# Gate weights loaded into the first attention's old tiles, and each weight's difference and sum as separate steps

## The chip, the cores and the metric

The kernel runs on one core of a Trainium2 chip. It is one launch that computes two transformer blocks. Its time is the device time of a whole execution in microseconds (us); 771.56 us is the median of three runs (771.15 to 772.16).

## The reference

`x` is 2 x 1024 tokens of 256 values. Two blocks follow each other, and in each the attention and the feed-forward part (ffn) read the same normalised input:

```python
xn = layernorm(x)
x = x + attn0(xn) + ffn0(xn)       # linear attention; ffn with ternary weights
xn = layernorm(x)
x = x + attn1(xn) + ffn1(xn)       # softmax attention, 16 heads, RoPE; Hadamard ffn
# ffn1:
x = fwht(x * SU_ug) / 64
up, gate = x @ W_up.T * ws[:1024] * 64, x @ W_gate.T * ws[1024:] * 64
x = fwht(silu(gate) * up * SU_dp) / 64
y = x @ W_down.T * (Wscale_dp * 64)
```

The Hadamard transform `fwht` of the input can be moved onto the weights: instead of transforming every token, the kernel transforms W_up and W_gate once (256 rows each, for 1024 outputs). A transform over 256 rows is one over 128 rows, done as a matmul with a 128x128 Hadamard matrix, of the sum and of the difference of the two halves of 128 rows. Sum and difference are what this change is about.

## The kernel before

**Precision.** Weights and activations are used as a rounded high part and the rest as a low part (names ending in H and L), so that a product is two or three matmuls. In ffn terms: a `gate` or `up` of the first ffn is four L748 matmuls of 512 columns into one PSUM bank, a `down` eight L754 matmuls of 256 columns into banks 6 and 7.

**Order.** There is no dynamic scheduling. `work_order` writes one list of pieces by hand; each engine walks through this list and does its part of each piece, and semaphores join them. The main line is the first ffn: four chunks of 512 tokens, in each of them m = 0 to 7 with `gate`, `up` and, three behind, `down`. A side line (`side0`) is woven in: first the first attention, then the preparation of the second block's weights (`prep_attn1`, `prep_down` 0 to 3, `prep_ug` 0 to 7), then the query and key projections of the second attention (`qk`). Preparation stands beside chunk 2 from m = 6 and chunk 3 up to m = 3 of the first ffn.

**One m of the first ffn.** TensorE `gate`; ScalarE tanh into `sg` (L1457); VectorE multiplies with the gate (L1239), which frees that bank; VectorE multiplies with `up` (L1248, "the product"), which frees the other; ScalarE copies into `hh` (L1465); GpSimd makes the low part `hl` (L1591, `low_part`); `down` reads both. Gates and ups rotate through the banks 3, 4, 5; the side line through 0, 1, 2.

**The preparation.** `prep_ug` u (L871 to L878) is one matmul with the Hadamard matrix, u = 0 to 3 for the up weights and 4 to 7 for the gate weights: two with the sum, two with the difference. ScalarE writes the high part UGH (L1445), VectorE the low part UGL (L1274), which frees the bank. Sum and difference are made on GpSimd by `halves_ug` (L1572 to L1581): both in one piece, difference (L1579) and sum (L1581, in place). `prep_attn1` (ScalarE, L1431) takes the high parts of the second attention's weights from the staging tile `stg[1]`, `low_attn1` (GpSimd, L1583 to L1587) their low parts, and signals `w1l`. The first `qk` waits for `w1l` to reach 2.

**Loads.** They go through SP's queue in the order of the list. `load_up` (L643) brings the up weights to `stg[0]`, once the down weights have left it. `load_gate` (L647) brings the gate weights to `stg[1]`, once `low_attn1` is done. `load_cs` (L633) is behind it and brings the tables for RoPE.

The order of the list around the change, ffn pieces with (chunk, m): `up` (2,5), `down` (2,2), `ln_norm` 5, `bias` (1,1), `att_b`, `gate` (2,6), `prep_attn1`, `up` (2,6), `prep_down` 0, `down` (2,3), `ln_turn` 5, `gate` (2,7), `prep_down` 1, `up` (2,7), `halves_ug` 0, `prep_down` 2, `down` (2,4), `low_attn1`, `load_gate`, `prep_down` 3, `down` (2,5), `prep_ug` 0, `down` (2,6), `down` (2,7), `halves_ug` 1, `prep_ug` 1, `ffn_end`, `gate` (3,0), `load_cs`, `prep_ug` 2, `up` (3,0), `prep_ug` 3, `gate` (3,1), `prep_ug` 4, `up` (3,1), `gate` (3,2), `prep_ug` 5, `up` (3,2), `prep_ug` 6, `gate` (3,3), `prep_ug` 7, `up` (3,3), `qk` 0, `down` (3,0), `ln_stats` 6.

Of the kernel before, what the change touches and what calls it, by code (L numbers as in the profile page):

```python
# [8 lines left out]
ALU = mybir.AluOpType  # L9
# [30 lines left out]
""".split()  # L40

DMAS = """
cols idn c ob wsd x0 x1 x2 x3 st0 st1 cs pad sp0 sp1 sp2 sp3 km0 km1 qm0 qm1 ks0 ks1 qs0 qs1 m0 m1
oe0 oe1 num0 num1 rc0 rc1 rs0 rs1 late0 late1 late2 late3 wl y
""".split()

# [19 lines left out]
def work_order():  # L66
# [3 lines left out]
    def put(*piece):  # L70
        order.append(piece)
# [139 lines left out]
    def side0():  # L211
        bf = 0
        for n, _ in enumerate(attention0()):
            if 14 <= n < 18:
                next(tn)
                if n == 17:
                    put("scales")
                    put("spread_vb")
                    put("load_wa1")
            if n == 18:  # L220
                put("fold")
            if n == 30:
                put("add_vb", ps.next())
            if n >= 18 and n % 3 == 1 and bf < 6:
                put("butterfly", bf)
                bf += 1
                if bf == 6:
                    put("load_up")
            yield
        ps.slots.append(2)  # L230
        put("prep_attn1")
        yield
        for q in range(4):
            put("prep_down", q, ps.next())
            yield
            if q == 1:
                put("halves_ug", 0)
            if q == 2:
                put("low_attn1")
                put("load_gate")  # L240
        for u in range(8):
            put("prep_ug", u, ps.next())
            yield
            if u == 0:
                put("halves_ug", 1)
        for c in (0, 1):
            for n in range(2):
                yield from qk(c, n, 4)
        put("load_m", 0)
        put("load_m", 1)  # L250
# [25 lines left out]
    for i in (1, 2):  # L276
        next(ln0[i])
    put("signs")
    sd0 = side0()
    next(sd0)  # L280
    next(ln0[2])
# [89 lines left out]
    st, mxr = Ring([0, 1, 2, 3]), Ring([4, 5, 6])  # L371
# [10 lines left out]
    while s < 8 * NP + LAG or any(k >= s for k in plan):  # L382
        live = s < 8 * NP
        for piece in plan.get(s, []):
            if piece[0] == "recip":
                p = piece[1]
# [21 lines left out]
        if 0 <= s - LAG < 8 * NP:  # L408
# [4 lines left out]
            elif t % 8 == 7:  # L413
                p = t // 8
# [18 lines left out]
def program(nc, x_d, wa0, tern, wa1, wo1, wf1, cols_d, bkv_d, cos_d, sin_d, had_d, mask_d, ident_d, pad_d, sel_d, wl_d, ob_d, wsd_d, y_d):  # L433
    with ExitStack() as ctx:
        base = -(-nc.sbuf_base // 32) * 32

        def sb(name, kb, shape, dt=F32):
            return nc.alloc_sbuf_tensor_at(name, shape, dt, offset=base + int(kb * KB))

        q = {n: ctx.enter_context(nc.semaphore(f"s_{n}")) for n in SEMAPHORES}  # L440
        d = {n: ctx.enter_context(nc.semaphore(f"d_{n}")) for n in DMAS}
# [4 lines left out]
        cols = sb("cols", 24, [128, NCOL])  # L446
# [14 lines left out]
        W1H = sb("W1H", 60, [128, 2, 768], F32R)  # L461
        W1L = sb("W1L", 66, [128, 2, 768], F32R)
        WOH = sb("WOH", 80, [128, 2, 256], F32R)
        WOL = sb("WOL", 82, [128, 2, 256], F32R)
# [21 lines left out]
        stg = [sb(f"stg{i}", 174 + 8 * i, [128, 2048]) for i in range(2)]  # L486
        XC = [sb(f"XC{i}", (190, 194, 156, 160)[i], [128, 4, 256]) for i in range(4)]
        XD = [sb(f"XD{i}", (16, 20, 198)[i], [128, 4, 256]) for i in range(3)]
        stg2 = sb("stg2", 190, [128, 2048])
        DIF = [sb(f"DIF{i}", (198, 190)[i], [128, 1024]) for i in range(2)]  # L490
        OB = sb("OB", 202, [128, 256])
        WSD = sb("WSD", 203, [128, 256])
        rz = [sb(f"rz{i}", 207 + i / 8, [128, 2, 8]) for i in range(2)]
# [37 lines left out]
        def r32(ap):  # L531
            return ap.bitcast(F32)
# [24 lines left out]
        def slot_value(p):  # L557
# [1 line left out]


        STAGE = {"wa0": (0, 16), "tern0": (1, 16), "tern1": (0, 32), "tern2": (1, 32), "down": (0, 48), "wa1": (1, 64),
                 "up": (0, 64), "gate": (1, 80)}

        def o_slots(p):

# [39 lines left out]
        def _(e):  # L605
# [39 lines left out]
                e.dma_start(stg[0][:, :], wf1[0]).then_inc(d["st0"], 16)  # L645

            def load_gate():  # L647
                e.wait_ge(q["w1l"], 2)
                e.dma_start(stg[1][:, :], wf1[1]).then_inc(d["st1"], 16)

            def qk_split(c, n):
                i = 2 * c + n
# [65 lines left out]
            def last(banks):  # L718
                for i in range(2):
                    for cc in range(2):  # L720
# [4 lines left out]
            parts = {f.__name__: f for f in (start, load_wa0, load_ob1, tern_abs, load_down, load_cs, load_wa1, load_up, load_gate, qk_split, load_m, load_s, max_rows,  # L725
                                             load_wl, out, recip, project, last)}
# [6 lines left out]
        def _(e):  # L733
# [134 lines left out]

            def prep_ug(u, b):
                n, k, h = u // 4, u // 2 % 2, u % 2  # L870
                src = DIF[n] if k else stg[n][:, 0:1024]  # L871
                claim(b)
                if h == 0:
                    e.wait_ge(q["hs"], 2 * n + 2)
                e.matmul(bank[b], HAD[:, :], src[:, h * 512:(h + 1) * 512], start=True, stop=True).then_inc(q["pu"], 1)
                freed[b] = q["ul"], u + 1
# [148 lines left out]
            def last(banks):  # L1025
# [32 lines left out]
                for i, qs in enumerate(halves):  # L1058
                    e.wait_ge(q["ll"], i + 1)
                    for cc in range(2):  # L1060
                        for r in range(2):
# [4 lines left out]
            parts = {f.__name__: f for f in (start, ln_turn, tern_scale, kv_in, kv_out, q0, att_n, att_t, att_b, add_vb, prep_down, prep_ug,  # L1066
                                             gate_a, gate, up_a, up, down_a, down, ffn_end, qk, v, max_half, max_rows, scores, values, project, last)}
# [312 lines left out]
        def _(e):  # L1380
# [94 lines left out]
            def qk_split(c, n):  # L1475
                i = 2 * c + n
                rot, spl = rots[c // 2], spls[c // 2]
                sc = 0.25 if n == 0 else 1.0
                for m in range(2):
                    e.wait_ge(q["rg"], 2 * i + m + 1)  # L1480
                    if i == 0:
                        e.wait_ge(q["pu"], 4)
                    else:
                        e.wait_ge(d[f"sp{2 * m}"], 32 * i)
                    e.activation(spl[2 * m][:, :], rot[m][:, :], ACT.Copy, scale=sc).then_inc(q["sh"], 1)  # L1485
# [30 lines left out]
            def last(banks):  # L1516
# [6 lines left out]
                for i, qs in enumerate(halves):  # L1523
# [3 lines left out]
            parts = {f.__name__: f for f in (start, ln_stats, ln_turn, w0h, tern_abs, kv_in, q0, att_t, prep_attn1, prep_down, prep_ug, gate, up,  # L1527
                                             hidden, qk_split, v, max_rows, scores, out, load_exp, last)}
# [5 lines left out]
        def _(e):  # L1534
# [34 lines left out]
                a, z = (x.rearrange("p (o t i) -> p o t i", t=2, i=256 << k // 2) for x in (pair if k // 2 % 2 == 0 else pair[::-1]))  # L1569
                e.tensor_tensor(z[:, :, k % 2, :], a[:, :, 0, :], a[:, :, 1, :], ALU.subtract if k % 2 else ALU.add).then_inc(q["bf"], 1)  # L1570

            def halves_ug(n):  # L1572

                i, value = STAGE["up" if n == 0 else "gate"]
                lo, hi = stg[i][:, 0:1024], stg[i][:, 1024:2048]
                e.wait_ge(d[f"st{i}"], value)
                if n == 1:
                    e.wait_ge(q["pd"], 4)
                e.tensor_tensor(DIF[n][:, :], lo, hi, ALU.subtract).then_inc(q["hs"], 1)  # L1579
                e.wait_ge(q["hs"], 2 * n + 1)  # L1580
                e.tensor_tensor(lo, lo, hi, ALU.add).then_inc(q["hs"], 1)  # L1581

            def low_attn1():  # L1583
                for i, (o, n, H, L) in enumerate(((0, 768, W1H, W1L), (1536, 256, WOH, WOL))):
                    raw = stg[1][:, o:o + 2 * n].rearrange("p (k n) -> p k n", k=2)
                    e.wait_ge(q["w1h"], i + 1)
                    e.tensor_tensor(L[:, :, :], raw, r32(H[:, :, :]), ALU.subtract).then_inc(q["w1l"], 1)  # L1587

            def low_part(f):
                e.wait_ge(q["hh"], f + 1)  # L1590
# [69 lines left out]
                    e.memset(DEN[1][96:128, :], 1.0).then_inc(q["fill"], 1)  # L1660
                    e.wait_ge(q["fill"], 2)

            parts = {f.__name__: f for f in (bias, fold, kv_in, q0, butterfly, low_attn1, halves_ug, up, hidden, ones_v, qk_join, load_wl, out, recip, times, high, low)}
            for name, *args in order:
                if name in parts:
                    parts[name](*args)
# [83 lines left out]
```

## Time and profile before

| | |
|---|---|
| median of three runs | 771.56 us (771.15 to 772.16) |
| the profiled execution | 771.74 us, of it 769.9 us span |
| TensorE matmuls busy | 705.2 us, 92% of the span |
| VectorE, ScalarE, GpSimd busy | 549.1, 434.9 and 299.3 us |
| chain that ended last | 59% TensorE |
| preparation of the ffn weights (`prep_ug` 0 to 7) | 204.7 to 228.2 us |
| mean granted clock | 0.965 of full speed |

Times in the rows are microseconds from the start of the span. An engine's busy time counts its instructions; matmuls overlap, so that the distance from one start to the next is shorter than the duration shown. In brackets stands the idle time before an instruction and what ended it. The granted clock is 1.00 at 2.4 GHz and 0.50 at 1.2 GHz.

### The profile page before, as it was taken

What the parts mean: (1) busy time and instruction counts of PE and PEld (TensorE: products, weight loads), DVE (VectorE), ACT (ScalarE), POOL (GpSimd) and SP (SyncE); (2) the same over time, 40 slices, a digit from 0 to 9 for tenths busy, and PEclk for the clock granted to TensorE, in tenths of its full rate; (3) what the DMA queues carried; (4) which work ended last, traced back from release to release, by engine and by line L of the source; (5) the groups of instructions that cost most, each with busy time, mean ns of one, the idle gap of its engine ahead of it and who ended that gap; (6) DMA issues with size and microseconds to landing.
All of it is one profiled execution on the core that took longest, in us unless ns stands there. A gap on an engine that the chain in (4) does not pass through costs nothing.

```text
span 769.9 us, 10969 instructions
## 1 busy us (share of the span) xinstructions
PE 705.2 (92%) x4186; PEld 442.3 (57%) x4186; DVE 549.1 (71%) x895; ACT 434.9 (56%) x579; POOL 299.3 (39%) x277
## 2 busy tenths in 40 slices
PE   3778898969687998999999998999999999999998
PEld 3657797958456777867767676333333433333345
DVE  4897766676368676667878888888888378888415
ACT  2542323344344554243233334899999899999883
POOL 0157865332644585354254343022233213422520
PEclk7798999998899999999999999999999999999999
DMA  6136101000021356342311102344344245342231
GB/s 250 55 114 228 55 1 55 1 1 0 19 91 44 122 187 201 107 148 70 111 55 56 56 5 69 110 139 136 107 138 139 91 134 172 123 138 84 78 102 59
DMA packets 25704, 74.14 MB, mean 96 GB/s; under 512 B 4604, under 2 KB 5980, under 8 KB 24692
## 3 DMA queue, kind: packets, MB, share of 16 engines
q1 hardware_dynamic: 21124, 65.37, 25.4%
q0 software_dynamic: 3808, 7.60, 3.3%
q8 instruction: 33, 0.54, 0.3%
q10 hardware_dynamic: 720, 0.48, 0.2%
q14 instruction: 19, 0.16, 0.1%
HBM read 54.54 MB, written 23.06 MB: 101 GB/s over the span
## 4 chain that ended last, share of the span: by engine, by line
PE 59%; POOL 2%; DVE 2%; ACT 2%; issue 1%; DMA 0%; SPq 0%; DVEq 0%; ACTq 0%; POOLq 0%
PE PS L1010 16%; PE PS L748 12%; PE PS L996 11%; PE PS L754 8%; PE PS L979 6%; PE PS L969 4%; DVE mx L1310 1%; POOL sg L1600 1%; ACT P L1503 1%; POOL rot L1620 0%; POOL rot L1621 0%; DMA scr_k<-spl 0%; PE PS L985 0%; ACT spl L1485 0%; ACT us L1468 0%
## 5 line engine op out<-in xcount | busy, mean ns | idle before, releaser
L1503 ACT ACTIVATE P<-PS 128x1024 f32<-128x1024 f32 x256 | 249.1, 1023 | 30.9 <-PE PS L996 30.6
L1317 DVE TENSOR_REDUCE mx<-PS 128x1 f32<-128x512 f32 x300 | 189.1, 682 | 33.2 <-PE PS L979 31.6
L1310 DVE TENSOR_REDUCE mx<-PS 128x2 f32<-128x1024 f32 x106 | 124.8, 1220 | 37.4 <-PE PS L969 37.1
L1591 POOL TENSOR_TENSOR hl<-sg,hh 128x512 fp32r<-128x512 f32 x64 | 83.4, 1304 | 140.0 <-ACT hh L1465 73.8
L1010 PE MATMUL PS<-P,VV 128*32 128x512 f32 x1024 | 137.3, 608 | 0.1
L996 PEld LDWEIGHTS PS<-QS,KS 64*128 64x128 f32 x512 | 48.6, 183 | 124.0 <-ACT P L1503 110.9
L996 PE MATMUL PS<-QS,KS 64*128 64x512 f32 x512 | 117.0, 456 | 2.3 <-DVE mx L1310 1.8
L979 PE MATMUL PS<-KM,QM 64*128 64x512 f32 x300 | 81.7, 398 | 0.0
L1459 ACT ACTIVATE sg<-PS,cols 128x512 f32<-128x512 f32 x32 | 22.0, 689 | 80.4 <-PE PS L748 80.4
L1600 POOL TENSOR_TENSOR sg<-sg,us 128x512 f32<-128x512 f32 x32 | 42.1, 1316 | 39.5 <-ACT us L1468 39.5
L748 PE MATMUL PS<-XH,UGH 128*128 128x512 f32 x128 | 54.3, 424 | 2.1 <-ACT sg L1459 1.1
L748 PE MATMUL PS<-XL,UGH 128*128 128x512 f32 x128 | 50.5, 394 | 0.0
L748 PE MATMUL PS<-XH,UGL 128*128 128x512 f32 x128 | 49.9, 390 | 0.0
L1465 ACT ACTIVATE hh<-sg 128x512 fp32r<-128x512 f32 x32 | 20.2, 630 | 51.5 <-DVE sg L1248 51.5
L1010 PEld LDWEIGHTS PS<-P,VV 128*32 128x32 f32 x1024 | 20.3, 108 | 39.8 <-issue 34.9
L1239 DVE SCALAR_TENSOR_TENSOR sg<-sg,PS 128x512 f32<-128x512 f32 x32 | 21.8, 682 | 26.6 <-ACT sg L1457 26.5
L969 PE MATMUL PS<-KM,QM 64*128 64x512 f32 x212 | 39.9, 448 | 0.8 <-DVE mx L1310 0.6
L979 PEld LDWEIGHTS PS<-KM,QM 64*128 64x128 f32 x300 | 38.2, 186 | 3.5 <-DVE mx L1317 0.6
L754 PE MATMUL PS<-DH,hh 128*128 128x256 f32 x128 | 38.0, 297 | 0.0
L1457 ACT ACTIVATE sg<-PS,s 128x512 f32<-128x512 f32 x32 | 21.8, 682 | 27.6 <-PE PS L748 27.5
L754 PE MATMUL PS<-DL,hh 128*128 128x256 f32 x128 | 36.2, 282 | 0.0
L754 PE MATMUL PS<-DH,hl 128*128 128x256 f32 x128 | 36.1, 282 | 0.0
(205 smaller groups left out, 1404.3 us busy)
## 6 DMA issues: line engine op xcount, KB each, us to landing
QM<-scr_q SPq DMA_DIRECT2D x16, 512.0 KB, 4.3
KM<-scr_k SPq DMA_DIRECT2D x16, 512.0 KB, 5.3
QS<-scr_q SPq DMA_DIRECT2D x16, 512.0 KB, 4.3
KS<-scr_k SPq DMA_DIRECT2D x16, 512.0 KB, 5.1
scr_q<-spl SPq DMA_DIRECT2D x24, 256.0 KB, 3.3
scr_k<-spl SPq DMA_DIRECT2D x24, 256.0 KB, 3.3
scr_o<-OE POOLq DMA_DIRECT2D x14, 256.0 KB, 2.8
stg<-in_tern SPq DMA_DIRECT2D x3, 1024.0 KB, 4.8
```

What stands on the lines that cost most here:

```text
L748: i = e.matmul(out, l, r, start=start and j == 0, stop=stop and j == len(pairs) - 1)
L754: i = e.matmul(out[:, r * 256:r * 256 + 256], l, x, start=first and r == 0 and j == 0, stop=last and j == len(pairs) - 1, skip_group_check ...
L969: e.matmul(bank[b + h], QM[p % 2][hr, qt * 128:(qt + 1) * 128], KM[p % 2][hr, chunk(half)], start=True, stop=True).then_inc(q["mt"], 1)
L979: e.matmul(bank[b], QM[p % 2][hr, qt * 128:(qt + 1) * 128], KM[p % 2][hr, chunk(half)], start=True, stop=True).then_inc(q["mt"], 1)
L996: i = e.matmul(bank[b + h], KS[p % 2][hr, kt * 128:(kt + 1) * 128], QS[p % 2][hr, chunk(half)], start=True, stop=True)
L1010: i = e.matmul(PS[32 * c:32 * c + 32, 7, :], v_head(8 * b + kt, 2 * j + c // 2), P[s % 4][:, chunk(c // 2 + 2 * (c % 2))], start=(kt == 0) ...
L1310: e.tensor_reduce(mx[p % 2][:, :, qt, half], PS[:, b:b + 2, :], AX.X, ALU.max).then_inc(q["mx"], 2)
L1317: e.tensor_reduce(mx[p % 2][:, h, qt, half:half + 1], bank[b], AX.X, ALU.max).then_inc(q["mx"], 1)
L1459: e.activation(s[:, :], bank[b], ACT.Silu, scale=col("wsg", m)).then_inc(q["t"], 1)
L1503: e.activation(P[s % 4][:, half * 1024:(half + 1) * 1024], PS[:, b:b + 2, :].rearrange("p b n -> p (b n)"), ACT.Exp).then_inc(q["ex"], 1)
L1591: e.tensor_tensor(hl[f % 4][:, :], sg[f % 3][:, :], r32(hh[f % 4][:, :]), ALU.subtract).then_inc(q["hl"], 1)
L1600: e.tensor_tensor(s[:, :], s[:, :], us[f % 4][:, :], ALU.mult).then_inc(q["h"], 1)
```

## The change

- `load_gate` moves to the place behind `prep_attn1`. It waits for eight of the first attention's query pieces and for all sixteen `att_n`, and brings the gate weights in two DMAs to two new tiles GR, at 128 to 132 and 136 to 140 KB, where tiles of the first attention lay. The second GR tile and the first are later overwritten by UGL, each after it has been read.
- `halves_ug` is split into `difference` n and `total` n, four steps. `difference` 0 stands ahead of `up` (2,6), `total` 0 ahead of `prep_down` 1, `difference` 1 ahead of `prep_down` 2 and `total` 1 ahead of `prep_ug` 0.
- The gate weights' difference goes into the second half of `stg[0]`, after `total` 0.
- `low_attn1` is split into two pieces: the one for W1L stands ahead of `prep_ug` 2 and the one for WOL ahead of `prep_ug` 6.
- The first high part of the queries, written over `stg[0]`, waits for eight `prep_ug` matmuls instead of four.

The number of instructions stays the same but for one more DMA.

```diff
--- before.py
+++ after.py
@@ -40,7 +40,7 @@
 """.split()
 
 DMAS = """
-cols idn c ob wsd x0 x1 x2 x3 st0 st1 cs pad sp0 sp1 sp2 sp3 km0 km1 qm0 qm1 ks0 ks1 qs0 qs1 m0 m1
+cols idn c ob wsd gr x0 x1 x2 x3 st0 st1 cs pad sp0 sp1 sp2 sp3 km0 km1 qm0 qm1 ks0 ks1 qs0 qs1 m0 m1
 oe0 oe1 num0 num1 rc0 rc1 rs0 rs1 late0 late1 late2 late3 wl y
 """.split()
 
@@ -229,20 +229,25 @@
             yield
         ps.slots.append(2)
         put("prep_attn1")
+        put("load_gate")
+        put("difference", 0)
         yield
         for q in range(4):
             put("prep_down", q, ps.next())
             yield
+            if q == 0:
+                put("total", 0)
             if q == 1:
-                put("halves_ug", 0)
-            if q == 2:
-                put("low_attn1")
-                put("load_gate")
+                put("difference", 1)
+            if q == 3:
+                put("total", 1)
         for u in range(8):
             put("prep_ug", u, ps.next())
             yield
-            if u == 0:
-                put("halves_ug", 1)
+            if u == 1:
+                put("low_attn1", 0)
+            if u == 5:
+                put("low_attn1", 1)
         for c in (0, 1):
             for n in range(2):
                 yield from qk(c, n, 4)
@@ -487,7 +492,9 @@
         XC = [sb(f"XC{i}", (190, 194, 156, 160)[i], [128, 4, 256]) for i in range(4)]
         XD = [sb(f"XD{i}", (16, 20, 198)[i], [128, 4, 256]) for i in range(3)]
         stg2 = sb("stg2", 190, [128, 2048])
-        DIF = [sb(f"DIF{i}", (198, 190)[i], [128, 1024]) for i in range(2)]
+        GR = [sb(f"GR{i}", (128, 136)[i], [128, 1024]) for i in range(2)]
+        HALF = [[stg[0][:, 0:1024], stg[0][:, 1024:2048]], [GR[0][:, :], GR[1][:, :]]]
+        DIF = [sb("DIF", 198, [128, 1024])[:, :], stg[0][:, 1024:2048]]
         OB = sb("OB", 202, [128, 256])
         WSD = sb("WSD", 203, [128, 256])
         rz = [sb(f"rz{i}", 207 + i / 8, [128, 2, 8]) for i in range(2)]
@@ -559,7 +566,7 @@
 
 
         STAGE = {"wa0": (0, 16), "tern0": (1, 16), "tern1": (0, 32), "tern2": (1, 32), "down": (0, 48), "wa1": (1, 64),
-                 "up": (0, 64), "gate": (1, 80)}
+                 "up": (0, 64)}
 
         def o_slots(p):
 
@@ -645,8 +652,10 @@
                 e.dma_start(stg[0][:, :], wf1[0]).then_inc(d["st0"], 16)
 
             def load_gate():
-                e.wait_ge(q["w1l"], 2)
-                e.dma_start(stg[1][:, :], wf1[1]).then_inc(d["st1"], 16)
+                e.wait_ge(q["qg"], 8)
+                e.wait_ge(q["an"], 16)
+                for i in range(2):
+                    e.dma_start(HALF[1][i], wf1[1][:, i * 1024:(i + 1) * 1024]).then_inc(d["gr"], 16)
 
             def qk_split(c, n):
                 i = 2 * c + n
@@ -868,7 +877,7 @@
 
             def prep_ug(u, b):
                 n, k, h = u // 4, u // 2 % 2, u % 2
-                src = DIF[n] if k else stg[n][:, 0:1024]
+                src = DIF[n] if k else HALF[n][0]
                 claim(b)
                 if h == 0:
                     e.wait_ge(q["hs"], 2 * n + 2)
@@ -1479,7 +1488,7 @@
                 for m in range(2):
                     e.wait_ge(q["rg"], 2 * i + m + 1)
                     if i == 0:
-                        e.wait_ge(q["pu"], 4)
+                        e.wait_ge(q["pu"], 8)
                     else:
                         e.wait_ge(d[f"sp{2 * m}"], 32 * i)
                     e.activation(spl[2 * m][:, :], rot[m][:, :], ACT.Copy, scale=sc).then_inc(q["sh"], 1)
@@ -1569,22 +1578,25 @@
                 a, z = (x.rearrange("p (o t i) -> p o t i", t=2, i=256 << k // 2) for x in (pair if k // 2 % 2 == 0 else pair[::-1]))
                 e.tensor_tensor(z[:, :, k % 2, :], a[:, :, 0, :], a[:, :, 1, :], ALU.subtract if k % 2 else ALU.add).then_inc(q["bf"], 1)
 
-            def halves_ug(n):
-
-                i, value = STAGE["up" if n == 0 else "gate"]
-                lo, hi = stg[i][:, 0:1024], stg[i][:, 1024:2048]
-                e.wait_ge(d[f"st{i}"], value)
-                if n == 1:
-                    e.wait_ge(q["pd"], 4)
-                e.tensor_tensor(DIF[n][:, :], lo, hi, ALU.subtract).then_inc(q["hs"], 1)
+            def difference(n):
+
+                if n == 0:
+                    e.wait_ge(d["st0"], STAGE["up"][1])
+                else:
+                    e.wait_ge(d["gr"], 32)
+                    e.wait_ge(q["hs"], 2)
+                e.tensor_tensor(DIF[n], HALF[n][0], HALF[n][1], ALU.subtract).then_inc(q["hs"], 1)
+
+            def total(n):
+
                 e.wait_ge(q["hs"], 2 * n + 1)
-                e.tensor_tensor(lo, lo, hi, ALU.add).then_inc(q["hs"], 1)
-
-            def low_attn1():
-                for i, (o, n, H, L) in enumerate(((0, 768, W1H, W1L), (1536, 256, WOH, WOL))):
-                    raw = stg[1][:, o:o + 2 * n].rearrange("p (k n) -> p k n", k=2)
-                    e.wait_ge(q["w1h"], i + 1)
-                    e.tensor_tensor(L[:, :, :], raw, r32(H[:, :, :]), ALU.subtract).then_inc(q["w1l"], 1)
+                e.tensor_tensor(HALF[n][0], HALF[n][0], HALF[n][1], ALU.add).then_inc(q["hs"], 1)
+
+            def low_attn1(i):
+                o, n, H, L = ((0, 768, W1H, W1L), (1536, 256, WOH, WOL))[i]
+                raw = stg[1][:, o:o + 2 * n].rearrange("p (k n) -> p k n", k=2)
+                e.wait_ge(q["w1h"], i + 1)
+                e.tensor_tensor(L[:, :, :], raw, r32(H[:, :, :]), ALU.subtract).then_inc(q["w1l"], 1)
 
             def low_part(f):
                 e.wait_ge(q["hh"], f + 1)
@@ -1660,7 +1672,7 @@
                     e.memset(DEN[1][96:128, :], 1.0).then_inc(q["fill"], 1)
                     e.wait_ge(q["fill"], 2)
 
-            parts = {f.__name__: f for f in (bias, fold, kv_in, q0, butterfly, low_attn1, halves_ug, up, hidden, ones_v, qk_join, load_wl, out, recip, times, high, low)}
+            parts = {f.__name__: f for f in (bias, fold, kv_in, q0, butterfly, low_attn1, difference, total, up, hidden, ones_v, qk_join, load_wl, out, recip, times, high, low)}
             for name, *args in order:
                 if name in parts:
                     parts[name](*args)
```

## Rows read from the trace of the kernel before

**Rows 1.** Who waited for whom, 195 to 230: us in total, times, longest.

```profile
PE PS L875 <- POOL stg L1581: 8.5, 2, 4.7
```

**Rows 2.** Timeline of TensorE: start, duration, engine, line, operation, [idle before <-releaser].

```profile
198.96 0.28 PE L754 MATMUL PS<-TD,hl 128*128 128x256 f32 x1
...
199.67 0.28 PE L754 MATMUL PS<-TD,hl 128*128 128x256 f32 x1
204.68 2.04 PE L875 MATMUL PS<-stg,HAD 128*128 128x512 f32 x2 [4.73 <-POOL stg L1581]
...
209.94 1.11 PE L875 MATMUL PS<-stg,HAD 128*128 128x512 f32 x2
...
211.81 1.02 PE L875 MATMUL PS<-DIF,HAD 128*128 128x512 f32 x2
...
213.60 1.02 PE L875 MATMUL PS<-DIF,HAD 128*128 128x512 f32 x2
...
219.28 1.10 PE L875 MATMUL PS<-stg,HAD 128*128 128x512 f32 x2 [3.73 <-POOL stg L1581]
...
228.99 0.39 PE L748 MATMUL PS<-XH,W1H 128*128 128x512 f32 x1
...
231.48 0.39 PE L748 MATMUL PS<-XH,W1L 128*128 128x512 f32 x1
```

**Rows 3.** Timeline of GpSimd in the same stretch.

```profile
190.03 2.38 POOL L1542 TENSOR_TENSOR X<-X,OB 128x1024 f32<-128x1024 f32 x1 [0.55 <-DVE XD L1115]
...
198.54 1.29 POOL L1591 TENSOR_TENSOR hl<-sg,hh 128x512 fp32r<-128x512 f32 x1 [4.60 <-ACT hh L1465]
199.78 2.34 POOL L1579 TENSOR_TENSOR DIF<-stg 128x1024 f32<-128x1024 f32 x1
...
204.50 3.44 POOL L1587 TENSOR_TENSOR W1L<-stg,W1H 128x1536 fp32r<-128x1536 f32 x1
...
214.34 2.38 POOL L1579 TENSOR_TENSOR DIF<-stg 128x1024 f32<-128x1024 f32 x1 [5.17 <-DMA stg<-in_wf]
216.79 2.35 POOL L1581 TENSOR_TENSOR stg<-stg 128x1024 f32<-128x1024 f32 x1
...
227.51 1.28 POOL L1591 TENSOR_TENSOR hl<-sg,hh 128x512 fp32r<-128x512 f32 x1 [2.77 <-ACT hh L1465]
```

**Rows 4.** Timelines of VectorE and ScalarE in the same stretch.

```profile
215.05 0.67 DVE L1248 TENSOR_TENSOR sg<-sg,PS 128x512 f32<-128x512 f32 x1
...
217.66 0.68 DVE L1239 SCALAR_TENSOR_TENSOR sg<-sg,PS 128x512 f32<-128x512 f32 x1
...
230.64 0.75 DVE L1290 SCALAR_TENSOR_TENSOR rot<-PS,cols,COS 128x512 f32<-128x512 f32 x1
...
215.76 0.63 ACT L1465 ACTIVATE hh<-sg 128x512 fp32r<-128x512 f32 x1 [2.19 <-DVE sg L1248]
216.29 0.67 ACT L1445 ACTIVATE UGH<-PS,s 128x512 fp32r<-128x512 f32 x1
216.86 0.68 ACT L1457 ACTIVATE sg<-PS,s 128x512 f32<-128x512 f32 x1
```

**Rows 5.** TensorE's last `att_n`, and the weight loads: KB, us to landing.

```profile
178.05 1.11 PE L830 MATMUL PS<-kvb,QP 128*128 128x136 f32 x4
...
stg<-in_wf SPq DMA_DIRECT2D x3, 1024.0 KB, 4.9
```

**Rows 6.** Two stops of TensorE, and stretches (the number after POOL is PEclk).

```profile
41.28 0.50 PE L748 MATMUL PS<-W0H,XH 128*128 128x512 f32 x1 [2.25 <-DVE QP L1202]
...
130.32 0.69 PE L813 MATMUL PS<-ve,zk 128*128 128x129 f32 x4 [2.23 <-DVE zk L1207]
...
42.00:43.00 1.00, 1.00 (x8) 0.82 (x7) 1.00 (x3) 0.00 (x0) 1.00 (x1) 1.00 0.00 0
...
132.00:133.00 1.00, 1.00 (x6) 1.00 (x6) 0.14 (x1) 0.69 (x1) 0.00 (x0) 0.50 0.00 0
```

**Rows 7.** Instructions of line 1303: count, ns min/median/max, first and last start.

```profile
L1303 DVE SCALAR_TENSOR_TENSOR spl<-rot,spl x16: 677/688/1772, 246.2 to 341.8; 128x512 fp32r<-128x512 f32 x16
```

## The prediction

> **What bounds the kernel now.** I read in this order: the page (TensorE is the engine with the most work), the list of who waited for whom, TensorE's instructions in order of time, then GpSimd's in the same stretch, then ScalarE's and VectorE's. The waits show one thing that is large and belongs to this change: TensorE waited 8.5 us, in two stops, for the sum of a weight's halves that GpSimd makes at L1581 [rows 1]. In TensorE's timeline these are the stops before `prep_ug` 0 (204.68, idle 4.73) and before `prep_ug` 4 (219.28, idle 3.73) [rows 2]. Both times TensorE had nothing else to do: the pieces stand in a fixed order. GpSimd's rows say why it was late. The first pair of halves starts at 199.78, straight behind the low part of 198.54, with no wait shown for its operand; it stands there only because the order puts it there. The second pair waits 5.17 us for a DMA [rows 3]: the gate weights go into the tile from which `low_attn1` still reads, so `load_gate` waits for it.
>
> Each stop costs more than its idle time, because the granted clock falls behind it. From where `prep_down` 3 and the `down` after it end (199.67 plus one pitch, 199.79) to `prep_ug` 1 (209.94) are 10.15 us. The work in between is `prep_ug` 0 and sixteen L754 matmuls. At full clock an L754 matmul takes 0.118 (198.96 to 199.67 are six pitches), a 512-column L748 matmul 0.23 (228.99 to 231.48 are eleven), and a `prep_ug` with four of those 1.79 (211.81 to 213.60), so `prep_ug` alone 0.87 [rows 2]. That makes 0.87 + 16 x 0.118 = 2.77. The first stop costs 10.15 - 2.77 = **7.38 us**. The same for the second: from the end of the slot that began at 213.60 (215.39) to the first matmul of `qk` (228.99) are 13.60; the work is four such slots and one group of four, 4 x 1.79 + 0.92 = 8.08; the cost is **5.52 us**, 3.89 of it standing and 1.62 at half clock.
>
> **Part 1: the up weights' halves are taken earlier.** `difference` 0 now stands behind `bias` (1,1), `total` 0 behind the low part that follows. GpSimd: the bias begins at 190.03 and takes 2.38; difference 2.34 to 194.7; the low part (1.28, the duration at 227.51) to 196.0; `total` 0 (2.35) to 198.3 [rows 3]. The low part that began at 198.54 is still free to begin there, so nothing on GpSimd moves behind it. `prep_ug` 0 is reached by TensorE at 199.79 and finds its operand 1.5 us old. What was delayed is one low part, by the difference's 2.34; its first reader is the `down` of chunk 2, m = 6, which TensorE reaches at 200.7. Its late end, 196.0, leaves 4.7 us of slack. The first stop goes: -7.38.
>
> **Part 2: the gate weights' load.** It now waits for the last `att_n` (TensorE, 178.05 plus 1.11) instead of for `low_attn1`; a weight of 1 MB lands 4.9 after its issue [rows 5], so its halves, now two DMAs, lie there from about 185, and twice that time would change nothing. On SP only `load_cs` is queued behind it, which today is issued behind the later gate load and so comes earlier too. `difference` 1 takes the place of today's first half step at 199.78 and `total` 1 ends at 204.5. TensorE's `prep_ug` 4, shifted, is due at 215.39 - 7.38 = 208.0: 3.5 us of slack. The second stop goes as well: -5.52. The tile of the gate difference is now the freed half of the up weights' tile, and ScalarE's first split waits for eight `prep_ug` matmuls instead of four; they lie ahead of `qk`, and the split behind it: nothing.
>
> **Part 3: what is late next.** I keep the old time axis from here (new time = old - 7.38). With no stop, TensorE would have done all before `qk` at 215.39 + 8.08 = 223.47. Two things stand in front of it. The PSUM banks come free along a chain that goes to and fro between VectorE and ScalarE. Its intervals are in the rows: VectorE's product of chunk 3, m = 0, (3,0) for short, at 215.05, the copy 0.71 later, UGH 0.53, the tanh 0.57, VectorE 0.80 [rows 4]; then 1.26 for that instruction and one low part of a `prep_ug`. So the product of (3,1) is at 218.92; the next, with one `prep_ug` copy fewer in front, at 222.14; that of (3,3) at 226.01. None of the banks that this frees is late for TensorE by more than the next item. That is **`low_attn1`'s second half**: it used to be done ahead of all this, now it stands on GpSimd behind the low part of (3,2), and `qk` waits for its semaphore. The copy of (3,2) begins at 222.85 and ends at 223.48, its low part runs from 223.56 to 224.84, the second half of `low_attn1` (128x512, the same 1.28) to 226.1, and TensorE follows such an end by 0.14 (216.79 + 2.35 against 219.28) [rows 2, 3]. `qk` starts at 226.22: a new stop of 2.75 us. The first half of `low_attn1` (3.44) fits between `total` 1 and the next low part, at 204.5 to 207.9 against 209.1 in new time: nothing.
>
> **The sum.** 7.38 + 5.52 - 2.75 = 10.15 on TensorE. On VectorE, which sets the pace behind `qk`: the first rotation began at 230.64 and now waits for the first six matmuls of `qk`, 226.22 + 1.36 and 0.17 of run-out, 227.75: 2.9 earlier, and 7.38 + 2.9 = 10.3. Both agree, so all four engines enter the rest 10.2 us earlier [rows 4]. There, I find nothing tied to an absolute time, so the gain stays.
>
> **The clock behind the new stop** is what the trace of before cannot show. An L748 matmul lasts 0.39 at a pitch of 0.23, so the rows would put 2.6 idle to this stop of 2.75. Up to 345 nine stops of over 2 us began at full clock; behind seven of them the clock fell to 1.2 GHz. The nearest are one of 2.23, behind which it fell (0.50 at 132), and one of 2.25, behind which it stayed (1.00 at 42) [rows 6]; all five longer ones (2.94, 3.08, 3.54, 3.73, 4.73) had a fall. So a fall is likelier than not. Its price lies between 0 and the 2.49 that half clock cost behind the first stop; I take the 1.6 of the second, the stop nearest in length and with the same kind of matmul. It hits the path: the second group of `qk` is what VectorE waits for. Net gain 10.2 - 1.6 = 8.6.
>
> The profiled execution took 771.74 (span 769.9, and 1.8 around it); the median of the runs is 0.18 below. 771.74 - 8.6 - 0.18 = **763.0 us**.
>
> **A rule against the move.** The longest VectorE instruction with both inputs in SBUF, L1303, has durations of 0.68 to 1.77 for one shape, so something disturbs it at times [rows 7]. The Trainium skill (GPSIMD Engine Reference, Key points) says that GpSimd shares its SBUF interfaces with VectorE and contends with VectorE instructions that have two SBUF inputs or run in a two-port mode. That rule would charge GpSimd's moved steps for what runs beside them. Beside them, at 192 to 208 and at 217 to 219 in new time, every VectorE instruction of the code has at most one tensor input in SBUF, so by the rule the sum stays as it is; were all VectorE instructions affected, the chain of part 3 would be drawn out, in the way of the second rival.
>
> **Rivals.**
> - *The clock holds at the new stop.* For it: the stop at 41.28, and that where a stop lies seems to matter as much as its length. Then the gain is 10.2: 761.4.
> - *More is given back.* The chain of part 3 gets 2 to 3 us longer (disturbed VectorE instructions at the layer norm behind `qk`, where GpSimd's low parts lie beside them), or one more fall of the clock (1.6) comes at a stop of about 2 us that had none. For it: the new order packs all four engines. Against: all instructions behind `qk` keep their order and distances. 8.6 - 2.3: 765.3.
> - *The new stop is shorter or absent.* If the low parts come faster than I chained them, the first rotation is bound by VectorE alone, 226.69 (the end of the product of (3,3)) against 230.64: 7.38 + 3.95 = 11.3, 760.2.
> - *Slower: the gate weights land late.* GpSimd waits for them at `difference` 1, ahead of `low_attn1` and four low parts, and TensorE behind it. This costs from a landing at 203.1 on (208.0 less 0.14, 2.38 and 2.35), one for one, and has eaten the gain when they land at about 213, since `low_attn1` (3.44 + 1.28) and the low parts then follow that wait; at today's 214.3 `qk` would come 1 to 2 us later than now: 773. Against: the wait ends with TensorE's instruction of 178.05, and the transfer would have to take 33 us instead of 5.
>
> **How the numbers follow.** Forecast (both stops gone, new stop, clock falls) 0.50; clock holds 0.29; more given back 0.12; stop absent 0.04; slower 0.02; the rest, 0.03, is that the gain is lost somewhere I do not see, near no change. Range: from the full gain with no new stop, 760.4, to the forecast with 2.5 for the clock and 1.9 more given back, 765.8. A measurement of this kernel can tell 0.2%, 1.5 us, from no change: faster 0.95, same 0.03, slower 0.02.
>
> **What will show it.** The wait of TensorE for `total` is gone, and `prep_ug` 0 to 7 stand 1.8 to 2.8 us apart with no stop over 1 us from 198 to 216. GpSimd's `difference` 0 starts at 192.4 and `difference` 1 at 199.8 with no wait for a DMA. TensorE stops for 2.6 us at the first L748 matmul with W1H, at about 216.1 to 218.8, released by GpSimd's step into WOL, and behind it the granted clock is 0.5 for some 3 us. From there, every row of before has its partner 8.6 us earlier. I am wrong if TensorE waits for banks among the `prep_ug` pieces, if the shift shrinks behind 262, or if `qk` finds its semaphore set.

## The result and the profile after

The changed kernel took **762.39 us** (median of four executions, 762.1 to 765.25) beside 771.84 for the kernel before (four executions, the 771.56 of the table above was the median of the first three): ratio 0.9887, 95% interval 0.9862 to 0.9912. In two later sets, on two chips, its medians were 764.81 and 764.71, with the ratios 0.9902 (0.988 to 0.9925) and 0.9913 (0.9899 to 0.9926). The forecast was 763.0, with 760.4 to 765.8 for the range.

TensorE in order of time, profile of the kernel after (765.25 us, the longest of the four; columns as in [rows 2], `prep_ug` is L884 here):

```profile
199.29 1.02 PE L884 MATMUL PS<-stg,HAD 128*128 128x512 f32 x2
...
202.06 1.02 PE L884 MATMUL PS<-stg,HAD 128*128 128x512 f32 x2
...
203.84 1.02 PE L884 MATMUL PS<-DIF,HAD 128*128 128x512 f32 x2
...
207.41 1.02 PE L884 MATMUL PS<-GR,HAD 128*128 128x512 f32 x2
...
213.66 1.02 PE L884 MATMUL PS<-stg,HAD 128*128 128x512 f32 x2
...
218.18 0.47 PE L757 MATMUL PS<-XH,W1H 128*128 128x512 f32 x1 [2.57 <-DVE UGL L1283]
...
219.20 0.63 PE L757 MATMUL PS<-XH,W1H 128*128 128x512 f32 x1
```

The rows of `prep_ug` 0 and 4 have no bracket: both stops of [rows 2] are gone. From `prep_ug` 0 to `prep_ug` 1 are 2.77 us where 5.26 lay, and before it nobody waits. A new stop of 2.57 stands ahead of the first query projection, and behind it a 512-column matmul lasts 0.63 instead of 0.39. Stretches of one microsecond around it (busy time of TensorE, its weight loads, VectorE, ScalarE and GpSimd, then the granted clock, as in [rows 6]):

```profile
218.00:219.00 1.00, 0.82 (x3) 0.71 (x4) 0.72 (x2) 0.25 (x1) 0.08 (x1) 0.82 0.00 0
219.00:220.00 1.00, 1.00 (x3) 0.76 (x3) 0.00 (x0) 0.98 (x2) 0.54 (x1) 0.50 0.00 0
220.00:221.00 1.00, 1.00 (x4) 0.75 (x3) 0.18 (x1) 0.69 (x1) 0.73 (x1) 0.50 0.00 0
221.00:222.00 1.00, 1.00 (x4) 0.81 (x3) 1.00 (x2) 0.00 (x0) 0.00 (x0) 0.50 0.00 0
222.00:223.00 1.00, 1.00 (x7) 0.86 (x7) 0.42 (x2) 0.00 (x0) 0.00 (x0) 0.97 0.07 16
```

It runs at 1.2 GHz for 3.4 of these five microseconds. GpSimd in the same profile, against [rows 3]:

```profile
191.86 2.35 POOL L1588 TENSOR_TENSOR DIF<-stg 128x1024 f32<-128x1024 f32 x1
...
195.41 2.39 POOL L1593 TENSOR_TENSOR stg<-stg 128x1024 f32<-128x1024 f32 x1
...
199.27 2.38 POOL L1588 TENSOR_TENSOR stg<-GR,GR 128x1024 f32<-128x1024 f32 x1
201.73 2.38 POOL L1593 TENSOR_TENSOR GR<-GR,GR 128x1024 f32<-128x1024 f32 x1
204.07 3.49 POOL L1599 TENSOR_TENSOR W1L<-stg,W1H 128x1536 fp32r<-128x1536 f32 x1
...
215.59 1.26 POOL L1603 TENSOR_TENSOR hl<-sg,hh 128x512 fp32r<-128x512 f32 x1 [1.93 <-ACT hh L1474]
216.81 1.27 POOL L1599 TENSOR_TENSOR WOL<-stg,WOH 128x512 fp32r<-128x512 f32 x1
```

The gate weights' difference begins at 199.27 with no wait for a DMA (5.17 before). The sum is ready at 204.11 and TensorE comes for it at 207.41. The last row is the second half of `low_attn1`: it ends at 218.08, and TensorE starts 0.10 later, although its own row names as the releaser VectorE's UGL, which ends at 218.12:

```profile
217.38 0.74 DVE L1283 SCALAR_TENSOR_TENSOR UGL<-PS,s,UGH 128x512 fp32r<-128x512 f32 x1
```

Which of the two it is, the first experiment decides.

**A ruler for the experiments.** Whole times of one kernel scatter by up to 4.9 us within a set (758.45 to 763.33 for `qk_first_low`), because the clock falls elsewhere too (below). So I measure a stretch in each profile: from ScalarE's copy into W1H, ahead of all that was changed, to VectorE's `BATCH_NORM_STATS2`, behind the query projection. In the kernel before:

```profile
188.60 1.48 ACT L1431 ACTIVATE W1H<-stg 128x1536 fp32r<-128x1536 f32 x1
...
233.29 1.39 DVE L1098 BATCH_NORM_STATS2 bst<-X 128x6 f32<-128x256 f32 x4
```

and in the kernel after:

```profile
188.09 1.47 ACT L1440 ACTIVATE W1H<-stg 128x1536 fp32r<-128x1536 f32 x1
...
224.13 1.40 DVE L1107 BATCH_NORM_STATS2 bst<-X 128x6 f32<-128x256 f32 x4
```

44.69 against 36.04: **8.65 us**, where the forecast's sum was 8.6. A second profile of the kernel before has 44.47, so a gain read with this ruler is good to about 0.2 us.

### The profile page after: what moved, and what is told of

The parts are those of the page before. It is cut to its first block, busy times and chain, and to the rows that moved or that the text cites. A ratio compares the mean times of both kernels' runs of the same rounds, so it can differ in the third digit from the quotient of the medians.

```text
span 763.4 us, 10971 instructions
## 1 busy us (share of the span) xinstructions
PE 705.0 (92%) x4186; PEld 441.2 (58%) x4186; DVE 549.6 (72%) x895; ACT 434.9 (57%) x579; POOL 298.5 (39%) x277
## 4 chain that ended last, share of the span: by engine, by line
PE 60%; POOL 2%; DVE 2%; ACT 2%; issue 1%; DMA 0%; SPq 0%; DVEq 0%; ACTq 0%; POOLq 0%
PE PS L1019 17%; PE PS L757 12%; PE PS L1005 11%; PE PS L763 8%; PE PS L988 6%; PE PS L978 4%; DVE mx L1319 1%; POOL sg L1612 1%; ACT P L1512 1%; POOL rot L1632 1%; POOL rot L1633 0%; DMA scr_k<-spl 0%; PE PS L994 0%; ACT spl L1494 0%; ACT us L1477 0%
## 5 line engine op out<-in xcount | busy, mean ns | idle before, releaser
L1477 ACT ACTIVATE us<-PS,cols 128x512 f32<-128x512 f32 x32 | 21.9, 685 | 24.8 <-PE PS L757 24.8
```

## The experiments

All kernels, with the stretch from their own two rows as above, the gain against 44.69, and the time of whole executions (one execution for "before, once more"):

| kernel | stretch, us | gain in it | median, us | ratio to before (95%) |
|---|---|---|---|---|
| before / before, once more | 44.69 / 44.47 | | 771.84 / 771.31 | |
| after | 36.04 | 8.65 | 762.39 | 0.9887 (0.9862 to 0.9912) |
| after, once more / in five rounds | 36.00 / 35.96 | 8.69 / 8.73 | 764.81 / 764.71 | 0.9902, 0.9913 |
| `qk_first_low` / in five rounds | 33.19 / 33.18 | 11.50 / 11.51 | 761.12 / 759.72 | 0.9853 (0.9818 to 0.9887), 0.9852 (0.9831 to 0.9873) |
| `after_filled` | 34.54 | 10.15 | 761.9 | 0.9868 (0.9845 to 0.9891) |
| `up_alone` | 40.39 | 4.30 | 767.49 | 0.9936 (0.9912 to 0.9961) |
| `gate_alone` | 40.36 | 4.33 | 766.56 | 0.9923 (0.9903 to 0.9943) |
| `gate_late` | 39.28 | 5.41 | 767.46 | 0.9948 (0.9927 to 0.9968) |
| `before_filled` | 44.55 | 0.14 | 773.46 | 1.0014 (1.0001 to 1.0026) |

**What sets the new stop: `qk_first_low`.**

```diff
 def qk(c, n, b0, b1):
...
                     if i == 0 and m == 0:
-                        e.wait_ge(q["w1l"], 2)
+                        e.wait_ge(q["w1l"], 1)
...
 def project(g, n, r, b):
                     claim(b)
+                    if g == 0 and n == 0:
+                        e.wait_ge(q["w1l"], 2)
```

> The changed kernel, in which the first query projection waits for the first half of low_attn1 alone (the part for W1L, which it reads); the wait for the second half (WOL) stands ahead of the first output projection. Theory (the new stop of 2.6 us is set by low_attn1's second half behind a low part on GpSimd): the stop ahead of the projection goes, its second group then waits a short while for the bank that VectorE frees last, the first rotation starts with VectorE free, 1.1 us earlier, and the clock does not fall there (1.6): 2.7 us under the changed kernel's 762.4, about 759.7. Rival (the trace names VectorE's UGL as the releaser of that stop, so banks set it): the stop stays 2.6 us and the time 762.4.

TensorE in this kernel, at the first projection and at its next stop:

```profile
215.24 0.39 PE L757 MATMUL PS<-XH,W1H 128*128 128x512 f32 x1
...
216.73 0.50 PE L757 MATMUL PS<-XH,W1H 128*128 128x512 f32 x1
...
226.00 0.50 PE L757 MATMUL PS<-XH,TG 128*128 128x512 f32 x1 [2.94 <-DVE sg L1250]
```

The stop is gone, and the second group starts 0.1 late, as the chain of banks says. So `low_attn1`'s second half set it, and the name in the row (UGL) was only another engine's end at nearly the same moment, 218.12 against 218.08. The stretch is 2.85 shorter than after's, 2.7 were expected; the median, 761.12, is 1.4 above the 759.7 that was expected, and its interval overlaps that of the first set of after. The stop at 226 was 1.6 long and is now 2.94: TensorE waits there for VectorE, which got earlier by less. Repeated beside the kernel after on one chip:

> The changed kernel whose first query projection waits for the first half of low_attn1 alone, in more rounds. Theory: 33.2 us in that stretch, so 2.8 us under the changed kernel on the same chip, apart from where the clock falls later: 760 to 762. Rival (what the stop gives back is lost at the next stop, which grew from 1.6 to 2.9 us and can bring a fall of its own): within 1 us of the changed kernel.

Its median was 759.72 (758.89 to 763.15), 5 us below the changed kernel there; the stretch explains 2.8 of them. The intervals of the two ratios do not overlap. It beats both kernels. In `first_low_5` the clock fell behind the longer stop (2.91 us, half clock from 226.8 on), in `qk_first_low` it did not (2.94 us), so the rival's mechanism exists. It does not eat the gain: the stretch to `BATCH_NORM_STATS2` is as short, and what lies behind it is compared further down.

**What half clock costs at the new stop: `after_filled`.**

```diff
                     if i == 0 and m == 0:
+                        for _ in range(9):
+                            e.matmul(bank[b], TU[:, 0, 0:128], XH[:, 0, chunk(3)], start=True, stop=True)
                         e.wait_ge(q["w1l"], 2)
```

> The changed kernel with nine matmuls of 512 columns, about 2.0 us, that fill the new stop ahead of the first query projection; their result is overwritten. Theory (behind that stop the clock falls, on the path, for 1.6 us): the clock stays at 2.4 GHz behind it, the rotations are 1.4 to 1.6 earlier, total 760.8 to 761.0. Rival (half clock there is covered by VectorE and ScalarE): 762.4 as without them, or a little more if the nine matmuls run past the wait.

```profile
215.20 2.23 PE L956 MATMUL PS<-XH,TU 128*128 128x512 f32 x9
217.93 0.50 PE L757 MATMUL PS<-XH,W1H 128*128 128x512 f32 x1 [0.50 <-POOL WOL L1601]
...
219.42 0.39 PE L757 MATMUL PS<-XH,W1H 128*128 128x512 f32 x1
```

The wait ends at the same place (here the row names WOL), but the matmuls behind it last 0.39. The stretch is 1.50 shorter: this is the price of the fall, on the path. 1.6 was forecast from the second stop of before. With 10.15 the stretch shows the sum without a fall as well, where 10.2 was forecast. The median of whole executions was expected at 760.8 to 761.0 and is 761.9, only 0.5 under after's first and 2.8 to 2.9 under its later ones; from those alone the price could not be read.

**Each part alone.** `up_alone` is the kernel before with `difference` 0 and `total` 0 at their new places, and the gate weights as they were:

```diff
         put("prep_attn1")
+        put("difference", 0)
         yield
...
-            if q == 1:
-                put("halves_ug", 0)
+            if q == 0:
+                put("total", 0)
```

> The kernel before with part 1 alone: the up weights' difference and sum early, everything of the gate weights as before (loaded into the staging tile after low_attn1). Theory: the first stop goes (7.4), but TensorE then comes to prep_ug 4 at 208.0, while the gate load, issued behind low_attn1 at about 204.5, lands at 209.5 and its sum is ready at 214.4: the second stop grows to 6.5 and 4.7 us of the gain are left, 767.1. Rival (the parts add up independently): 7.4 gained, 764.4.

```profile
202.74 1.30 POOL L1596 TENSOR_TENSOR WOL<-stg,WOH 128x512 fp32r<-128x512 f32 x1
208.88 2.35 POOL L1588 TENSOR_TENSOR DIF<-stg 128x1024 f32<-128x1024 f32 x1 [4.84 <-DMA stg<-in_wf]
...
213.79 2.04 PE L876 MATMUL PS<-stg,HAD 128*128 128x512 f32 x2 [6.21 <-POOL stg L1590]
```

The first stop went and the second grew from 3.73 to 6.21: measured from W1H, TensorE came 7.5 earlier to `prep_ug` 4 and the gate load, bound to `low_attn1`, only 5. Of 7.4 us 4.30 are left in the stretch, where 4.7 were expected. `gate_alone` is the kernel after with the up halves, `low_attn1` and the gate halves in their old places:

```diff
-        put("difference", 0)
...
-            if q == 0:
-                put("total", 0)
             if q == 1:
-                put("difference", 1)
-            if q == 3:
-                put("total", 1)
+                put("difference", 0)
+                put("total", 0)
+            if q == 2:
+                put("low_attn1", 0)
+                put("low_attn1", 1)
...
-            if u == 1:
-                put("low_attn1", 0)
-            if u == 5:
-                put("low_attn1", 1)
+            if u == 0:
+                put("difference", 1)
+                put("total", 1)
```

> The changed kernel with part 2 alone: the gate weights loaded early into the new tiles, but the up weights' two halves, both parts of low_attn1 and the gate weights' two halves on GpSimd in the old order and places. Theory: the first stop stays with its clock fall, the second goes (TensorE 5.5 earlier at the projection), and VectorE, bound by its chain with ScalarE, starts its rotations at 226.7 instead of 230.6: 3.9 gained, 767.9; no new stop. Rival (each stop is worth what it cost in the trace): 5.5 gained, 766.3.

The stretch gained 4.33, between the 3.9 of the chain and the 5.5 of the rival and nearer the first; the whole time, 766.56, is nearer the rival's figure, but by what happens outside the stretch. The trace decides it. TensorE needs 8.05 us from where it is ready for `prep_ug` 4 (215.34) to the projection (223.39), 13.60 in the kernel before: it gained the 5.5. VectorE did not. Its last product and its first rotation:

```profile
225.98 0.68 DVE L1255 TENSOR_TENSOR sg<-sg,PS 128x512 f32<-128x512 f32 x1
226.57 0.74 DVE L1297 SCALAR_TENSOR_TENSOR rot<-PS,cols,COS 128x512 f32<-128x512 f32 x1
```

The rotation follows the product with no wait and comes 4.3 earlier than in the kernel before, each measured from W1H. So the chain sets it, as the theory says, with 0.4 more gained than was worked out. Together the parts alone give 8.63 and the change 8.65. That they add up is chance: together they gain 11.5 (`qk_first_low`), and the order of the change gives 2.85 of it back.

**Where the load's landing begins to matter: `gate_late`.**

```diff
                 e.wait_ge(q["an"], 16)
+                e.wait_ge(q["ul"], 1)
```

> The changed kernel whose gate load waits, in addition, for the first UGL of VectorE (201.8), so that it lands at about 206.8 instead of 185. Theory (a landing after 203.1, or 202.6 on this kernel's own axis, costs one for one at prep_ug 4): a stop of about 4.4 us there, the chain behind it 3.4 later: 765.8 to 767.4, the larger if the clock falls behind it. Rival (the load's place does not matter as long as it is before the old 214): no change, 762.4.

```profile
207.55 2.36 POOL L1589 TENSOR_TENSOR stg<-GR,GR 128x1024 f32<-128x1024 f32 x1 [7.78 <-DMA GR<-in_wf]
...
212.47 2.05 PE L885 MATMUL PS<-GR,HAD 128*128 128x512 f32 x2 [4.45 <-POOL GR L1594]
```

Landing 5 us behind the point from which it was worked out to matter (202.6), the load makes a stop of 4.45, as expected; the stretch is 3.24 longer than after's, since the stop ahead of the projection shrinks from 2.57 to 1.01. The time is 767.46, just above the 765.8 to 767.4 that were expected. That is the mechanism of the prediction's slower rival, with a smaller delay. It is one landing time: that it costs nothing up to 202.6 was not measured.

**Are the falls at the old stops worth 4.1 us? `before_filled`.**

```diff
                 claim(b)
+                if u in (0, 4):
+                    for _ in range(14 if u else 18):
+                        e.matmul(bank[b], TU[:, 0, 0:128], XH[:, 0, chunk(3)], start=True, stop=True)
                 if h == 0:
                     e.wait_ge(q["hs"], 2 * n + 2)
```

> The kernel before with the two stops filled by matmuls whose result is overwritten: eighteen of 512 columns ahead of prep_ug 0 and fourteen ahead of prep_ug 4. It still waits as long, but TensorE is busy. Theory (2.5 and 1.6 us of the two stops' cost are half clock behind them): the clock stays at 2.4 GHz from 200 to 229; the 2.5 behind the first stop comes back in part only, because GpSimd and the load of the gate weights set when the second stop ends, and the 1.6 behind the second as far as VectorE's chain allows: 0.8 to 1.6 gained, 770.2 to 771.0. Rival (each fall is paid in full): 4.1 gained, 767.7.

```profile
200.24 4.27 PE L875 MATMUL PS<-XH,TU 128*128 128x512 f32 x18
205.13 1.12 PE L878 MATMUL PS<-stg,HAD 128*128 128x512 f32 x2 [0.62 <-POOL stg L1584]
208.00 1.02 PE L878 MATMUL PS<-stg,HAD 128*128 128x512 f32 x2
...
213.35 3.36 PE L875 MATMUL PS<-XH,TU 128*128 128x512 f32 x14
219.53 1.34 PE L878 MATMUL PS<-stg,HAD 128*128 128x512 f32 x2 [2.81 <-POOL stg L1584]
```

The first fall was prevented: `prep_ug` 1 comes 2.87 behind `prep_ug` 0, 5.26 before. But TensorE only reached the second stop that much earlier; its end is set by the gate load and did not move. The fourteen matmuls were used up 2.81 before it, and the clock fell behind it as before. Nothing is left in the stretch (0.14), and both theories expected more. So preventing a fall gains nothing ahead of a stop whose end is fixed. The whole time is 1.7 us longer than before by the medians (1.1 by the ratio). In the profiled execution the surplus lies where the attention begins: the clock is at half for 6.8 us there (479 to 487) and for 3.4 in the kernel before (479 to 484), and what lies behind the stretch is 1.6 longer. Why the fall is longer in this kernel is open.

**Why whole times scatter.**

> The changed kernel once more. Its first profiled execution took 765.25 and three others 762.1 to 762.6. Theory (the difference is two more stretches of half clock at stops that the kernel before has too, and where the clock falls differs from execution to execution): this profile shows another set of stretches at half clock, and its time is 762.4 plus or minus what they make, 1 to 1.2 us for each. Rival (the changed order costs 2.6 us behind 262 whenever it runs): the same losses at the same places in every profile.

> The changed kernel in more rounds, beside the next one on the same chip. Theory (gain of 8.6 us in the stretch from ScalarE's W1H copy to the layer norm behind the query projection, the rest spread by where the clock falls): 762 to 765 us, ratio to the kernel before 0.987 to 0.991, and the same 36.0 us in that stretch. Rival (the change costs something behind 262): the median lies above 765.

> The kernel before once more, for its profile. Theory (where the clock falls outside the two stops of this change differs from execution to execution in this kernel too): 44.7 us from the W1H copy to the layer norm behind the projection as in the first profile, with both falls, while one or more of the other stretches at half clock lie elsewhere or have another length; 771 to 774.6. Rival (the kernel before has one fixed set of falls and only the changed one varies): the same list of stretches, 771.7.

Three profiles of the changed kernel agree within 0.1 us in the stretch (36.04, 36.00, 35.96), but their executions took 765.25, 762.54 and 764.71. The median of `after_5` is inside the expected 762 to 765, its ratio of 0.9913 just above the expected 0.991. The stretches at half clock differ between the three, so the rival of `after_again` is out. One place where they part is a stop of 2.1 us that all of them have and the kernel before has too (292.40 there). The same instruction and the stretches behind it, first in `after_again`:

```profile
283.19 0.39 PE L757 MATMUL PS<-W1H,XH 128*128 128x256 f32 x1 [2.09 <-ACT VV L1500]
...
284.00:285.00 1.00, 1.00 (x7) 0.82 (x6) 0.34 (x1) 0.39 (x1) 1.00 (x1) 1.00 0.99 356
```

and in `after_5`:

```profile
284.04 0.39 PE L757 MATMUL PS<-W1H,XH 128*128 128x256 f32 x1 [2.10 <-ACT VV L1500]
...
285.00:286.00 1.00, 1.00 (x4) 0.81 (x4) 0.18 (x1) 0.39 (x1) 1.00 (x1) 0.50 1.00 334
```

The stop is the same to 0.01 us; in one execution the clock stays, in the other it falls. The profile shown first has this fall and a longer one where the attention begins (half clock from 472 to 478), and it lost 2.7 of the 9.2 us by which it led at 224. The kernel before had no fall at the 2.1 us stop in either of its two profiles, but in its second one a fall near the start of the span (42 to 46) that the first did not have, and not the two that the first had at 80 and 131; its times went from 770.69 to 774.63 over the sets. So it varies as well.

All twelve profiles together show what these falls cost. From `BATCH_NORM_STATS2` on, the order of the work is the same in all kernels (half clock in the last microsecond of the span is left out):

| profile | from there to the end of the span, us | half clock in it |
|---|---|---|
| `gate_alone` | 535.5 | 233 to 237 |
| `up_alone` | 536.2 | 474 to 478 |
| before, once more | 536.4 | 479 to 483 |
| `qk_first_low` | 536.5 | 467 to 471 |
| before | 536.6 | 479 to 484 |
| after, once more | 536.7 | 470 to 474 |
| `after_filled` | 536.9 | 282 to 287 |
| `before_filled` | 538.2 | 479 to 487 |
| after, in five rounds | 538.3 | 284 to 289, 472 to 476 |
| after | 539.3 | 283 to 287, 471 to 479 |
| `first_low_5` | 539.5 | 226 to 231, 281 to 285, 469 to 476 |
| `gate_late` | 539.6 | 287 to 291, 475 to 483 |

Profiles with the same falls agree within 0.6 us, whatever was changed. So apart from the falls the change costs nothing behind the stretch that these profiles could show. Against `gate_alone`, the one profile with no late fall, the fall at the 2.1 us stop costs about 1.4 us, a short one where the attention begins about 1 and a long one about 2.7. But the fall at the 2.1 us stop came in five of the eight profiles of kernels that derive from the one after and in none of the four others. Whether the change makes this fall likelier, or this is chance, these profiles cannot tell. That the second and third medians of the changed kernel are both some 2.4 us over the first may be this stop.

## Why the prediction was right

- **The cost of the two stops** (7.38 and 5.52, idle time and half clock together, 12.90). From where TensorE is ready for `prep_ug` 0 to the first projection it needs 29.20 us in the kernel before and 16.16 in `qk_first_low`: 13.04. By themselves they came out at 7.5 (`up_alone`) and 5.55 (`gate_alone`). In the stretch `qk_first_low` gained 11.50; the forecast for a kernel with no new stop, bound there by VectorE, was 11.3.
- **What is late next.** The new stop was put at 2.75 between starts, 2.6 by the measure of the rows; it is 2.57, at the instruction and behind the step that were named. `qk` was due at 218.84, and came at 218.18; 0.51 of that was there before the change (W1H at 188.09 instead of 188.60) and leaves 0.15.
- **The clock behind it.** It fell in all three profiles of the changed kernel, as seven of nine comparable stops had suggested, at 1.50 on the path instead of 1.6. That count left out a stop of 4.30 at 9.14, which had a fall too, so it is eight of ten.
- **The chain between VectorE and ScalarE.** The products of (3,0) to (3,3) came at 207.08, 210.95, 214.17 and 218.04: distances of 3.87, 3.22 and 3.87, the same as worked out from [rows 4].
- **The load.** No wait for it. `gate_late`, 5 us behind the point that was worked out, cost 4.45 in TensorE's stop and 3.24 in the stretch; it bears out the point only as far as one landing time can.
- **The rule of the Trainium skill** on the shared SBUF interfaces (GPSIMD Engine Reference, Key points) charged nothing here, and the stretch agrees: sum and measurement meet within the 0.2 us of the ruler without such a cost, and VectorE's and ScalarE's distances are those of before. No run here puts the moved steps beside VectorE instructions with two SBUF inputs.
- **What was wrong.** That "the gain stays" behind 262 held in `after_again`, not in every execution: 2.7 us went in the first profile, and a shift that shrinks behind 262 was one of the prediction's own signs of being wrong. The second rival named one more fall at a stop of about 2 us and gave all of its kind 0.12. In the three profiles of this kernel it came twice, so this chance was too small. All five longer stops of before had a fall, but the one of 2.94 in `qk_first_low` had none. The low end of the range, 760.4, should be 760.2, which the same text gives for the full gain with no new stop.
- **What was luck.** The stretch was forecast by its terms, the rest of the time only by supposing that nothing changes there. That the first median lies 0.6 from the forecast rests on three executions of 762.1 to 762.55 in a set of four; against the medians of the later two sets, 764.81 and 764.71, the single figure is 1.8 us too low, though inside the range, and they lie nearer the 765.3 of the second rival.

## What to carry to other kernels

When a stop goes, walk the next pieces of every engine at the new pace before counting its gain: here a wait on a semaphore that counted two steps, of which the reader needed one, gave back 2.85 of 11.5 us, and could be read off the order beforehand. Of two stops in a row, what is gained at the first is lost again at the second if its end is fixed (`before_filled`: 2.4 us gained, 0.1 left), and part of it if that end moves by less (`up_alone`: 4.30 left of 7.4). Compare variants over a stretch between two named instructions in each profile; the whole time of this kernel moves by 4 to 5 us from one execution to the next, and the part of it behind the stretch went along with where the clock fell.

## What was not expected of the hardware

A stop of TensorE that is the same to 0.01 us can end with the clock at 2.4 GHz or at 1.2: 2.09 us stayed in `after_again`, 2.10 us fell in `after_5`. The shorter of two can be the one that falls: 2.94 us stayed in `qk_first_low`, 2.91 fell in `first_low_5`. And filling most of a stop need not hold the clock: nine matmuls that left 0.50 us idle and eighteen that left 0.62 held it, fourteen that left 2.81 did not. Nothing between 0.62 and 2.81 was run.
